# Building the slot table of a routed expert stage: 64 small indirect transfers, or one-hot rows summed by TensorE

## The chip, the cores and the metric

The kernel runs on one core of one Trainium2 chip. The metric is the device time of one execution in microseconds, median of several runs.

## The reference

The reference is a small language-model tower of two layers over 8 sequences of 512 tokens, with 256 features: an embedding, and in each layer an attention and a feed-forward block with experts. Only the second layer's feed-forward block matters here. Its arguments are 8 routed experts and one shared expert, all of the same form.

```
top-2 of the 8 router scores per token, with two gates (a softmax of the two scores)
y = x + shared(norm(x)) + sum over the token's two experts of gate * expert(norm(x))
expert(z) = (silu(z @ w1) * (z @ w3)) @ w2          z: 256, hidden: 512
```

The kernel does not compute every expert on every token. It sorts the 8192 (token, expert) pairs by expert into 72 tiles of 128 places, each expert beginning a new tile, and runs an expert on its tiles alone. The **slot table** says which token stands at place p of tile m, and a second table holds that pair's gate. A place without a pair holds a filler: a token number of 4096 or more, whose result is not added, and gate 0.

## The kernel before, in words

The five engines run programs of their own, written out by hand for each stage; semaphores order them, and between stages all engines meet. The stages of this block are three.

- **Routing** (`route`): normalizes all tokens, writes the normalized rows to device memory, computes the router's scores and the choice as one-hot rows `hot`, and the gates `first` and `second`. SP also writes a blank slot table to device memory here (`empty`, 72 fillers a partition).
- **Shared expert** (`shared_expert`): 16 steps of 256 tokens. On PE a step is `hidden(i)`, four blocks of 12 matmuls with 256 columns (reduced float32, in three passes of split operands) into the two halves of `psG`, and `down(i)`, 24 such matmuls into `psY`. ACT applies silu, DVE multiplies (line 2052) and splits, ACT rounds, and DVE adds `psY` to the residual in `add(i)` (line 2061). The order on PE is `hidden(i)`, `down(i-1)`, `hidden(i+1)`; on DVE `gated(i)`, `add(i-1)`, `gated(i+1)`. A block of `hidden` waits until DVE has multiplied the block two before it. Steps in the middle are loops of two steps on PE, ACT and DVE.
- Inside the shared expert, `Sort` computes on DVE, between steps, where each pair goes: `dve_scan` after `gated(0)`, `dve_slots` after `add(0)`, and `dve_plan` (which weights are due when) after `add(1)`. `dve_slots` ends in a cast of 64 slot numbers a partition to integers, `sloti`. POOL then sends 64 indirect transfers (`pool_scatter`, line 1824), each of which writes 128 entries (token, gate) of 8 bytes to their places of the table in device memory.
- **Routed experts** (`routed_experts`): SP first reads the table back (`listed`, line 2143) and then the first expert's weights (two transfers of 1.5 MB, line 2153). DVE copies `listed` as float32, PE transposes it, DVE writes `table` and `gate` (lines 2332 to 2336). Then 72 tiles: POOL gathers the tile's rows from device memory, PE turns them and multiplies by the expert's weights, and POOL adds the result into the output with an indirect transfer (line 2175), tile after tile.

At the start of the shared stage DVE waits for POOL's constants (`pool_constants`), and PE for DVE's `both`.

Of the kernel before, what the change touches and what calls it, by code (L numbers as in the profile page):

```python
# [17 lines left out]
P = 128  # L18
F32 = mybir.dt.float32
# [9 lines left out]
NT = B * S // P  # L29
# [1622 lines left out]
def ffn_swiglu(nc, a, res, ident, dram, s_soft):  # L1652
# [5 lines left out]
    with ExitStack() as ctx:  # L1658
# [3 lines left out]
        load_plan = k.sb("load_plan", [1, 2, E1N], I32)  # L1662
        with ExitStack() as ctx1:
# [5 lines left out]
            shared_expert(nc, a["out"], res, ident, xh, xl, hot, first, second, w_h, w_l, weights_due, weights_at, load_plan, dram, s_soft)  # L1669
        routed_experts(nc, a["out"], ident, weights_due, weights_at, load_plan, dram, s_soft)  # L1670


def route(nc, a, res, ident, xh, xl, hot, first, second, w_h, w_l, dram, s_soft):

    with ExitStack() as ctx:
# [4 lines left out]
        empty = k.sb("empty", [P, TILES, 2], I32)  # L1680
        s = {n: k.sem(n) for n in "raw hi wt bias share none filler empty blank".split()}
# [5 lines left out]
        def _(sp):  # L1687
# [6 lines left out]
            sp.wait_ge(s["empty"], 3)  # L1694
            sp.dma_start(dram["table"].rearrange("(p m) c -> p m c", p=P), empty[:]).then_inc(s["blank"], 16)
# [8 lines left out]
            sp.wait_ge(s["blank"], 17)  # L1704
            sp.wait_ge(turn.s["stored"], 16 * B + 1)

        @block.gpsimd
        def _(pool):
            split_weights(pool, [router.w], s["raw"], s["hi"], s["wt"])
            router.pool_names(pool)  # L1710
            pool.memset(none[:], 0.0).then_inc(s["none"], 1)

            pool.iota(empty[:, :, 0], [[0, TILES]], base=B * S, channel_multiplier=1).then_inc(s["empty"], 1)
            pool.memset(empty[:, :, 1], 0).then_inc(s["empty"], 1)
# [47 lines left out]
class Sort:  # L1762


    PAD = NT // 2

    def __init__(self, k, hot, gates, weights_due, weights_at, load_plan, dram, s_soft):
        self.hot, self.due, self.at, self.load_plan, self.dram, self.soft = hot, weights_due, weights_at, load_plan, dram, s_soft
# [13 lines left out]
        self.sloti = k.sb("sloti", [P, 2, NT], I32)  # L1782
# [9 lines left out]
        self.entry = k.sb("entry", [P, NT, 2, 2], I32)  # L1792
        self.gates = gates
        self.ps = k.ps("psS", [P, 2, NT * E])
        names = "fixed parts both ranked sorted ready slots".split()
        self.s = {n: k.sem("sort_" + n) for n in names}

    def pool_constants(self, pool):
# [38 lines left out]
    def dve_both(self, dve):  # L1837
        dve.wait_ge(self.s["parts"], 8)
        for n in range(2):
            dve.tensor_copy(self.entry[:, :, n, 1].bitcast(F32), self.gates[n][:]).then_inc(self.s["slots"], 1)  # L1840
# [29 lines left out]
    def dve_slots(self, dve, n):  # L1870
# [21 lines left out]
        dve.tensor_copy(self.sloti[:], self.slotf[:]).then_inc(s["slots"], 1)  # L1892
# [59 lines left out]
def shared_expert(nc, out, res, ident, xh, xl, hot, first, second, w_h, w_l, weights_due, weights_at, load_plan, dram, s_soft):  # L1952

    TT = 256
    NTT = B * S // TT
    with ExitStack() as ctx:
        k = Kit(nc, ctx, "ffn1b")
        sort = Sort(k, hot, (first, second), weights_due, weights_at, load_plan, dram, s_soft)
# [21 lines left out]
        def _(pool):  # L1980
            sort.pool_constants(pool)
            sort.pool_scatter(pool)

        @block.tensor
        def _(pe):
# [29 lines left out]
            with pe.Fori(0, NTT // 2 - 1) as i:  # L2015
                hidden(2 * i + 1, 1)
# [438 lines left out]
```

## Time and profile before

| what | value |
|---|---|
| median of 3 runs | 1915.01 us (1912.12 to 1915.68) |
| the profiled execution | 1910.06 us |
| its span, first to last instruction | 1908.2 us |
| mean granted TensorE clock | 0.863 of full speed |
| PE busy | 1335.6 us (70%) |
| DVE busy | 1011.3 us (53%) |
| POOL busy | 721.1 us (38%) |
| ACT busy | 635.0 us (33%) |

Times are microseconds from the start of the span. PE is TensorE's matmul, PEld its loading of weights, which overlaps PE; DVE is VectorE, ACT ScalarE, POOL GpSimd, SP the engine that issues most transfers. Busy time is the time in which an engine's instructions run; idle time in a row is what lay before the instruction, with the instruction that ended it. A busy share of the span says how much an engine does, and not whether anyone waits for it.

### The profile page before, as it was taken

The page shows a single profiled execution, that of the slowest core. Times are in us where ns is not written, and L with a number is a line of the kernel's source. Part 1 is how long each engine was busy: PE and PEld are TensorE (multiplying, and loading weights), DVE is VectorE, ACT ScalarE, POOL GpSimd, SP SyncE. Part 2 cuts the span into 40 slices and gives each one's busy share as a digit, 9 for nine tenths or more (in the row PEclk, how much of TensorE's full clock was granted, in tenths as well). Part 3 has the DMA queues.
Part 4 walks back from the last instruction along what each step waited for, and adds up shares of the span by engine and source line. Part 5 has one row for each costly group of instructions (what it writes and reads, how often), then busy time and mean ns, then how long its engine had stood idle before and what let it go on. Part 6 is the DMA issues. An engine that isn't in the chain of part 4 may idle for free. (4 is left out here: it accounts for less than half of the span.)

```text
span 1908.2 us, 32827 instructions
## 1 busy us (share of the span) xinstructions
PE 1335.6 (70%) x9797; PEld 1053.7 (55%) x9798; DVE 1011.3 (53%) x1870; ACT 635.0 (33%) x1271; POOL 721.1 (38%) x596
## 2 busy tenths in 40 slices
PE   0466646999999746534442399646699699999997
PEld 0255533555555544323331267534689578888886
DVE  0688854666767274557778255463544233333332
ACT  0032222565656412223221044212234234333342
POOL 6166662555554001113445500200174135444454
PEclk9788776999999878867766599867799899999999
DMA  1023337999998000023323254022001363444431
GB/s 28 18 77 111 112 114 154 246 252 256 244 255 227 7 6 0 0 61 110 110 78 100 64 113 92 10 83 76 10 25 33 120 216 55 115 113 115 112 55 26
DMA packets 161663, 190.87 MB, mean 100 GB/s; under 512 B 27028, under 2 KB 137052, under 8 KB 161604
## 3 DMA queue, kind: packets, MB, share of 16 engines
q1 hardware_dynamic: 133044, 129.24, 24.6%
q0 software_dynamic: 28560, 60.91, 12.7%
q8 instruction: 29, 0.48, 0.1%
q14 instruction: 30, 0.25, 0.0%
HBM read 112.89 MB, written 78.25 MB: 100 GB/s over the span
## 5 line engine op out<-in xcount | busy, mean ns | idle before, releaser
L1122 DVE TENSOR_REDUCE att_top<-att_psA 128x2 f32<-128x1024 f32 (+8 forms) x256 | 245.3, 986 | 186.4 <-PE att_psA L998 118.5
L1092 ACT ACTIVATE att_prob<-att_psB 128x512 f32<-128x512 f32 (+4 forms) x464 | 231.7, 536 | 137.4 <-PE att_psB L1017 71.3
L2175 POOL DMA_INDIRECT out<-ffn1c_y,ffn1c_table x72 | 114.2, 1585 | 179.8 <-ACT ffn1c_y L2288 106.0
L997 PE MATMUL att_psA<-att_ka,att_qa 96*128 96x384 bf16 (+3 forms) x512 | 126.3, 312 | 31.5 <-POOL att_mask_kNone L913 30.3
L1016 PE MATMUL att_psB<-att_qa,att_ka 98*128 98x256 bf16 (+3 forms) x512 | 128.0, 303 | 4.7 <-ACT att_prob L1092 2.2
L1050 PE MATMUL att_psO<-att_prob,att_vu 128*32 128x128 f32 (+7 forms) x1408 | 106.0, 405 | 35.1 <-ACT att_prob L1092 35.0
L2316 DVE TENSOR_TENSOR ffn1c_hid<-ffn1c_psG,ffn1c_sil 128x512 f32<-128x512 f32 x72 | 49.8, 691 | 144.4 <-PE ffn1c_psG L2216 144.4
L2216 PE MATMUL ffn1c_psG<-ffn1c_w_h,ffn1c_xh 128*128 x288 | 97.8, 421 | 10.8 <-DMA ffn1c_w_l<-experts_lo 3.8
L998 PE MATMUL att_psA<-att_mask_qNone,att_idb 128*128 128x128 bf16 x512 | 101.7, 226 | 0.0
L2164 POOL DMA_INDIRECT ffn1c_rows<-normed_rows,ffn1c_table x72 | 70.9, 984 | 78.0 <-DVE ffn1c_gate L2336 53.8
L1050 PEld LDWEIGHTS att_psO<-att_prob,att_vu 128*32 128x32 f32 x1408 | 51.1, 109 | 85.7 <-issue 64.1
L1017 PE MATMUL att_psB<-att_mask_kNone,att_idb 128*128 128x128 bf16 x512 | 98.2, 220 | 0.0
L532 PE MATMUL qkv_psQ<-qkv1p_w_qk_hi,qkv_xTh 128*128 128x512 f32 x64 | 28.9, 544 | 96.8 <-DVE qkv_xTl L703 96.8
L2216 PE MATMUL ffn1c_psG<-ffn1c_w_h,ffn1c_xl 128*128 x288 | 91.8, 401 | 0.0
L2216 PE MATMUL ffn1c_psG<-ffn1c_w_l,ffn1c_xh 128*128 x288 | 91.2, 398 | 0.0
L997 PEld LDWEIGHTS att_psA<-att_ka,att_qa 96*128 96x128 bf16 x512 | 50.9, 101 | 64.5 <-POOL att_mask_kNone L913 30.7
L1824 POOL DMA_INDIRECT slots<-ffn1b_entry,ffn1b_sloti x64 | 64.3, 1004 | 46.5 <-DVE ffn1b_sloti L1892 27.3
L1016 PEld LDWEIGHTS att_psB<-att_qa,att_ka 98*128 98x128 bf16 x512 | 49.8, 97 | 44.1 <-ACT att_prob L1092 25.1
L2307 DVE TENSOR_TENSOR ffn1c_xl<-ffn1c_psX,ffn1c_xh 128x256 fp32r<-128x256 f32 x72 | 30.5, 424 | 82.3 <-ACT ffn1c_xh L2266 82.3
L532 PEld LDWEIGHTS qkv_psQ<-qkv1p_w_qk_hi,qkv_xTh 128*128 128x128 f32 x64 | 16.7, 275 | 102.4 <-DVE qkv_xTl L703 98.9
L234 POOL CAST out_w_o_hi<-out_w_o_raw 128x512 fp32r<-128x512 f32 x2 | 1.2, 610 | 189.4 <-DMA out_w_o_raw<-in_w_o 189.4
L2280 ACT CAST ffn1c_hh<-ffn1c_psH 128x512 fp32r<-128x512 f32 x72 | 42.3, 587 | 88.4 <-PE ffn1c_psH L2227 88.4
(365 smaller groups left out, 3742.8 us busy)
## 6 DMA issues: line engine op xcount, KB each, us to landing
prep_raw<-in_w_all POOLq DMA_DIRECT2D x27, 512.0 KB, 6.9
experts_hi<-prep_hi POOLq DMA_DIRECT2D x27, 512.0 KB, 3.6
experts_lo<-prep_lo POOLq DMA_DIRECT2D x27, 512.0 KB, 4.3
ffn1c_w_h<-experts_hi SPq DMA_DIRECT2D x8, 1536.0 KB, 6.8
ffn1c_w_l<-experts_lo SPq DMA_DIRECT2D x8, 1536.0 KB, 11.0
qkv_near<-near_keys SPq DMA_DIRECT2D x32, 320.0 KB, 4.4
v_rows<-qkv_vaug SPq DMA_DIRECT2D x8, 1024.0 KB, 4.6
att_vu<-v_rows SPq DMA_DIRECT2D x32, 256.0 KB, 3.7
```

What stands on the lines that cost most here:

```text
L997: pe.matmul(out, q, ka[0:KROWS, u.buf, h, 0:cols], start=True, stop=True)
L998: return pe.matmul(out[:, cols - P:cols], idb[:], mask_q[w][:], start=False, stop=True, skip_group_check=True)
L1016: pe.matmul(out, keys, qs, start=True, stop=True)
L1017: return pe.matmul(out[:, 0:P], idb[:], mask_k[w][:], start=False, stop=True, skip_group_check=True)
L1050: mm = pe.matmul(psO[VW * h:VW * (h + 1), P * j:P * j + have], vu[:, v.buf, j, h, :], prob[:, v.par, h, j, 0:have], start=(j == 0), stop=( ...
L1092: act.activation(dst, src, ACT.Exp, scale=0.25).then_inc(s["exp"], 1)
L1122: dve.tensor_reduce(dst, src, AX.X, ALU.max).then_inc(s["max"], 1)
L1824: pool.indirect_dma_start(out=self.dram["table"], in_=self.entry[:, t, n, :], in_offset=None, out_offset=bass.IndirectOffsetOnAxis(ap=self ...
L2164: pool.indirect_dma_start(out=rows[:, t.buf, :], out_offset=None, in_=dram["rows"], in_offset=bass.IndirectOffsetOnAxis(ap=table[:, t.valu ...
L2175: pool.indirect_dma_start(out=rows_out, in_=y[:, t.buf, :], in_offset=None, out_offset=bass.IndirectOffsetOnAxis(ap=table[:, t.value:t.val ...
L2216: mm = pe.matmul(psG[:, t.par, g, :], x[:, t.par, P * c:P * (c + 1)], w[:, bass.ds(at, 1), col:col + F1], start=(q == 0), stop=(q == 5))
L2316: dve.tensor_tensor(hid[:, t.par, :], psG[:, t.par, 1, :], sil[:, t.par, :], ALU.mult).then_inc(s["act"], 1)
```

## The change

The slot table no longer passes through device memory. Every pair's slot is split into a tile number `high` and a lane `low` (slot = 128 x tile + lane; rounding is done by adding and taking off a large constant). For each of the 64 columns of pairs DVE makes a one-hot row of 128 lanes and a one-hot row of 72 tiles, and multiplies the tile row by the token number (less 4096) and by the gate. PE multiplies the two and sums over all columns into one tile of PSUM, `psE`, 128 lanes by 2 x 72; DVE then adds 4096 and writes `table` and `gate`. This is done in 8 parts of 8 columns: DVE makes part 0 after `add(1)` and parts 1 to 7 after `add(3)` to `add(9)`, PE sums part c between `hidden(c+5)` and `down(c+4)`, and DVE reads the sum after `add(12)`. The plan moves from behind `add(1)` to behind `add(2)`.

Taken out are the blank table and its transfer in the routing stage, POOL's 64 transfers, the reading back, and the two transposes with their copies. POOL makes two more constants. The loops of the shared stage on PE and DVE are written out; ACT's stays.

The diff, cut to its core:

```diff
 class Sort:
     PAD = NT // 2
+    PART = 8
+    PARTS = 2 * NT // PART
+    WHOLE = 12582912.0
...
-        pool.iota(self.entry[:, :, :, 0], [[P, NT], [0, 2]], base=0, channel_multiplier=1).then_inc(s["parts"], 1)
-        pool.wait_ge(s["parts"], 8)
-
-    def pool_scatter(self, pool):
-        pool.wait_ge(self.s["slots"], 4)
-        for t in range(NT):
-            for n in range(2):
-                pool.indirect_dma_start(out=self.dram["table"], in_=self.entry[:, t, n, :], in_offset=None,
-                                        out_offset=bass.IndirectOffsetOnAxis(ap=self.sloti[:, n, t:t + 1], axis=0)
-                                        ).then_inc(self.soft["entries"], 16)
-        pool.wait_ge(self.soft["entries"], 16 * 2 * NT)
+        pool.iota(self.entry[:, :, 0], [[0, 2], [P, NT]], base=-B * S, channel_multiplier=1,
+                  allow_small_or_imprecise_dtypes=True).then_inc(s["parts"], 1)
+        pool.iota(self.lanes[:], [[1, P]], base=0, channel_multiplier=0,
+                  allow_small_or_imprecise_dtypes=True).then_inc(s["parts"], 1)
+        pool.iota(self.tiles[:], [[1, TILES]], base=0, channel_multiplier=0,
+                  allow_small_or_imprecise_dtypes=True).then_inc(s["parts"], 1)
+        pool.wait_ge(s["parts"], 10)
+
+    def dve_held(self, dve, c):
+        at = slice(self.PART * c, self.PART * (c + 1))
+        shape = [P, self.PART, TILES]
+        if c >= 1:
+            dve.wait_ge(self.s["held"], c + 1)
+        dve.tensor_tensor(self.tile_hot[:], self.tiles[:].unsqueeze(1).to_broadcast(shape),
+                          self.high[:, 2, at].unsqueeze(2).to_broadcast(shape), ALU.is_equal).then_inc(self.s["tile"], 1)
+        if c >= 2:
+            dve.wait_ge(self.s["placed"], c)
+        shape = [P, self.PART, P]
+        dve.tensor_tensor(self.lane_hot[:, c % 2], self.lanes[:].unsqueeze(1).to_broadcast(shape),
+                          self.low[:, at].unsqueeze(2).to_broadcast(shape), ALU.is_equal).then_inc(self.s["lane"], 1)
+        dve.wait_ge(self.s["tile"], c + 2)
+        shape = [P, self.PART, 2, TILES]
+        dve.tensor_tensor(self.held[:, c % 2], self.tile_hot[:].unsqueeze(2).to_broadcast(shape),
+                          self.entry[:, at, :].unsqueeze(3).to_broadcast(shape), ALU.mult).then_inc(self.s["held"], 1)
+
+    def pe_place(self, pe, c):
+        pe.wait_ge(self.s["lane"], c + 2)
+        pe.wait_ge(self.s["held"], c + 2)
+        for n in range(self.PART):
+            mm = pe.matmul(self.psE[:].rearrange("p v m -> p (v m)"), self.lane_hot[:, c % 2, n, :],
+                           self.held[:, c % 2, n].rearrange("p v m -> p (v m)"), start=(c == 0 and n == 0),
+                           stop=(c == self.PARTS - 1 and n == self.PART - 1), skip_group_check=True)
+        mm.then_inc(self.s["placed"], 1)
+
+    def dve_table(self, dve):
+        dve.wait_ge(self.s["placed"], self.PARTS + 1)
+        dve.tensor_scalar(self.table[:], self.psE[:, 0, :], float(B * S), None, ALU.add).then_inc(self.s["ready"], 1)
+        dve.tensor_copy(self.gate[:], self.psE[:, 1, :]).then_inc(self.s["ready"], 1)
+        dve.wait_ge(self.s["ready"], 6)
...
-        dve.tensor_copy(self.sloti[:], self.slotf[:]).then_inc(s["slots"], 1)
+        slot = self.slotf[:].rearrange("p c t -> p (c t)")
+        dve.tensor_scalar(self.high[:, 0], slot, 1.0 / P, 0.5 / P - 0.5, ALU.mult, ALU.add).then_inc(s["slots"], 1)
+        dve.wait_ge(s["slots"], 4)
+        dve.tensor_scalar(self.high[:, 1], self.high[:, 0], self.WHOLE, None, ALU.add).then_inc(s["slots"], 1)
+        dve.wait_ge(s["slots"], 5)
+        dve.tensor_scalar(self.high[:, 2], self.high[:, 1], -self.WHOLE, None, ALU.add).then_inc(s["slots"], 1)
+        dve.wait_ge(s["slots"], 6)
+        dve.scalar_tensor_tensor(self.low[:], self.high[:, 2], -float(P), slot, ALU.mult, ALU.add).then_inc(s["slots"], 1)
+        dve.wait_ge(s["slots"], 7)
...
 def shared_expert
...
+    LATE = 5
...
             hidden(0, 0)
-            with pe.Fori(0, NTT // 2 - 1) as i:
-                hidden(2 * i + 1, 1)
-                down(2 * i, 0)
-                hidden(2 * i + 2, 0)
-                down(2 * i + 1, 1)
-            hidden(NTT - 1, 1)
-            down(NTT - 2, 0)
+            for i in range(1, NTT):
+                hidden(i, i % 2)
+                if 0 <= i - LATE < sort.PARTS:
+                    sort.pe_place(pe, i - LATE)
+                down(i - 1, 1 - i % 2)
             down(NTT - 1, 1)
...
             gated(2, 0)
             add(1, 1)
-            sort.dve_plan(dve, n)
-            with dve.Fori(1, NTT // 2 - 1) as i:
-                gated(2 * i + 1, 1)
-                add(2 * i, 0)
-                gated(2 * i + 2, 0)
-                add(2 * i + 1, 1)
-            gated(NTT - 1, 1)
-            add(NTT - 2, 0)
+            sort.dve_held(dve, 0)
+            for i in range(3, NTT):
+                gated(i, i % 2)
+                add(i - 1, 1 - i % 2)
+                if i == 3:
+                    sort.dve_plan(dve, n)
+                if 1 <= i - LATE + 2 < sort.PARTS:
+                    sort.dve_held(dve, i - LATE + 2)
+                if i == LATE + sort.PARTS:
+                    sort.dve_table(dve)
             add(NTT - 1, 1)
...
 def routed_experts
...
-            sp.dma_start(listed[:], dram["table"].rearrange("(m p) c -> m p c", p=P)).then_inc(s["listed"], 16)
...
-            pe.wait_ge(s["slots"], 3)
-            for c in range(2):
-                mm = pe.transpose(psX[:, P * c:P * c + TILES], slots[:, c, :], ident[0:TILES, 0:TILES])
-            mm.then_inc(s["slotsT"], 1)
-            pe.wait_ge(s["table"], 3)
...
-            dve.wait_ge(s["listed"], 17)
-            dve.tensor_copy(slots[:, 0, :], listed[:, :, 0]).then_inc(s["slots"], 1)
-            dve.tensor_copy(slots[:, 1, :], listed[:, :, 1].bitcast(F32)).then_inc(s["slots"], 1)
-            dve.wait_ge(s["slotsT"], 2)
-            dve.tensor_copy(table[:], psX[:, 0:TILES]).then_inc(s["table"], 1)
-            dve.tensor_copy(gate[:], psX[:, P:P + TILES]).then_inc(s["table"], 1)
-            dve.wait_ge(s["table"], 3)
```

## Rows read from the trace of the kernel before

**Rows 1.** Windows: PE, PEld, DVE, ACT, POOL busy us, granted clock, DMA share, GB/s.
```profile
1349.00:1504.50 155.50, 145.43 (x1154) 143.44 (x1154) 71.74 (x187) 56.14 (x136) 64.27 (x64) 0.96 0.09 26
1504.50:1523.20 18.70, 1.84 (x7) 0.90 (x7) 2.27 (x7) 0.74 (x2) 5.77 (x6) 0.60 0.62 222
...
1375.30:1377.00 1.70, 1.67 (x14) 1.67 (x15) 0.76 (x2) 1.07 (x4) 1.09 (x1) 1.00 0.00 0
...
1390.00:1392.00 2.00, 2.00 (x12) 2.00 (x11) 0.76 (x2) 0.61 (x2) 1.39 (x3) 0.50 0.01 1
```

**Rows 2.** View of line 1824, POOL: instructions, duration, first and last start.
```profile
L1824 POOL DMA_INDIRECT slots<-ffn1b_entry,ffn1b_sloti x64: 963/967/1379, 1375.8 to 1458.3; - x64
```

**Rows 3.** Chain that ended last, in order of time: start, length, what.
```profile
1511.50 11.44 DMA ffn1c_w_l<-experts_lo
...
1557.84 6.90 DMA ffn1c_w_h<-experts_hi
...
1649.56 10.93 DMA ffn1c_w_l<-experts_lo
```

**Rows 4.** Timeline of DVE, shared stage: start, length, instruction, idle before and releaser.
```profile
1371.33 0.69 DVE L2061 TENSOR_TENSOR m_res<-m_res,ffn1b_psY 128x512 f32<-128x512 f32 x1 [1.58 <-PE ffn1b_psY L2007]
...
1374.85 0.42 DVE L2052 TENSOR_TENSOR ffn1b_act_f<-ffn1b_psG,ffn1b_sil 128x256 f32<-128x256 f32 x1
...
1381.41 0.69 DVE L2061 TENSOR_TENSOR m_res<-m_res,ffn1b_psY 128x512 f32<-128x512 f32 x1 [1.45 <-PE ffn1b_psY L2007]
...
1382.16 0.74 DVE L1912 TENSOR_TENSOR ffn1b_past<-ffn1b_ends,ffn1b_number 1x576 f32<-1x576 f32 x1
1382.83 0.20 DVE L1913 TENSOR_TENSOR ffn1b_pick<-ffn1b_ends,ffn1b_number 1x64 f32<-1x64 f32 x1
...
1386.72 0.22 DVE L1944 TENSOR_TENSOR ffn1b_which<-ffn1b_which,ffn1b_rounds 1x72 f32<-1x72 f32 x1
...
1387.80 0.42 DVE L2052 TENSOR_TENSOR ffn1b_act_f<-ffn1b_psG,ffn1b_sil 128x256 f32<-128x256 f32 x1 [0.45 <-DVE ffn_load_plan L1948]
...
1466.48 0.69 DVE L2061 TENSOR_TENSOR m_res<-m_res,ffn1b_psY 128x512 f32 x1 [1.48 <-PE ffn1b_psY L2007]
1468.92 0.42 DVE L2052 TENSOR_TENSOR ffn1b_act_f<-ffn1b_psG,ffn1b_sil 128x256 f32<-128x256 f32 x1 [1.76 <-ACT ffn1b_sil L2033]
...
1475.54 0.69 DVE L2061 TENSOR_TENSOR m_res<-m_res,ffn1b_psY 128x512 f32 x1 [1.48 <-PE ffn1b_psY L2007]
...
1484.12 0.69 DVE L2061 TENSOR_TENSOR m_res<-m_res,ffn1b_psY 128x512 f32 x1 [1.48 <-PE ffn1b_psY L2007]
```

**Rows 5.** Timeline of PE, shared stage.
```profile
1375.33 0.51 PE L1995 MATMUL ffn1b_psG<-ffn1s_xh,ffn1s_w_h 128*128 x2 [1.24 <-DVE ffn1b_act_f L2052]
...
1388.28 0.51 PE L1995 MATMUL ffn1b_psG<-ffn1s_xh,ffn1s_w_h 128*128 x2 [4.12 <-DVE ffn1b_act_f L2052]
...
1392.76 0.63 PE L2007 MATMUL ffn1b_psY<-ffn1s_w_h,ffn1b_act_h 128*128 128x256 f32 x4
...
1466.15 0.40 PE L1995 MATMUL ffn1b_psG<-ffn1s_xh,ffn1s_w_h 128*128 x2
```

**Rows 6.** Timeline of SP's queue at the start of the expert stage.
```profile
1509.59 0.34 SPq L2143 DMA_DIRECT2D ffn1c_listed<-slots  x1
1511.01 0.40 SPq L2153 DMA_DIRECT2D ffn1c_w_h<-experts_hi  x1
```

**Rows 7.** Timeline of POOL, then DVE, at the start of the shared stage.
```profile
1347.95 0.16 POOL L1812 IOTA ffn1b_thresholds<- 128x32 f32 x1
...
1348.20 0.28 POOL L1817 IOTA ffn1b_entry<- 128x64 int32 x1
...
1348.51 0.20 DVE L1840 COPY ffn1b_entry<-ffn_first 128x32 f32<-128x32 f32 x1 [4.41 <-POOL ffn1b_entry L1817]
```

**Rows 8.** Timeline of PE's weight loads in the embedding stage.
```profile
54.27 0.19 PEld L164 LDWEIGHTS emb_psO<-emb_w_blk,emb_rowsT 128*128 128x128 f32 x1 [0.24 <-issue]
54.70 0.19 PEld L164 LDWEIGHTS emb_psO<-emb_w_blk,emb_rowsT 128*128 128x128 f32 x1 [0.24 <-issue]
```

More of the change, by code:

```diff
@@ L1662, in ffn_swiglu @@
         load_plan = k.sb("load_plan", [1, 2, E1N], I32)
+        table, gate = k.sb("table", [P, TILES], I32), k.sb("gate", [P, TILES])
         with ExitStack() as ctx1:
@@ L1668, in ffn_swiglu @@
             route(nc, a, res, ident, xh, xl, hot, first, second, w_h, w_l, dram, s_soft)
-            shared_expert(nc, a["out"], res, ident, xh, xl, hot, first, second, w_h, w_l, weights_due, weights_at, load_plan, dram, s_soft)
-        routed_experts(nc, a["out"], ident, weights_due, weights_at, load_plan, dram, s_soft)
+            shared_expert(nc, a["out"], res, ident, xh, xl, hot, first, second, w_h, w_l, table, gate, weights_due, weights_at, load_plan, s_soft)
+        routed_experts(nc, a["out"], ident, table, gate, weights_due, weights_at, load_plan, dram, s_soft)
 def route(nc, a, res, ident, xh, xl, hot, first, second, w_h, w_l, dram, s_soft):
@@ L1679, in route @@
         none = k.sb("none", [P, D])
-        empty = k.sb("empty", [P, TILES, 2], I32)
-        s = {n: k.sem(n) for n in "raw hi wt bias share none filler empty blank".split()}
+        s = {n: k.sem(n) for n in "raw hi wt bias share none filler".split()}
         router.weights_there = s["wt"], 2
@@ L1791, in __init__ @@
         self.plan = k.sb("plan", [1, 2, E])
-        self.entry = k.sb("entry", [P, NT, 2, 2], I32)
+        self.entry = k.sb("entry", [P, 2 * NT, 2])
         self.gates = gates
         self.ps = k.ps("psS", [P, 2, NT * E])
-        names = "fixed parts both ranked sorted ready slots".split()
+        self.psE = k.ps("psE", [P, 2, TILES])
+        names = "fixed parts both ranked sorted ready slots lane tile held placed".split()
         self.s = {n: k.sem("sort_" + n) for n in names}
@@ L1837, in dve_both @@
     def dve_both(self, dve):
-        dve.wait_ge(self.s["parts"], 8)
+        dve.wait_ge(self.s["parts"], 10)
         for n in range(2):
-            dve.tensor_copy(self.entry[:, :, n, 1].bitcast(F32), self.gates[n][:]).then_inc(self.s["slots"], 1)
+            dve.tensor_copy(self.entry[:, NT * n:NT * (n + 1), 1], self.gates[n][:]).then_inc(self.s["slots"], 1)
         dve.tensor_tensor(self.both[:], self.hot[:, 0], self.hot[:, 1], ALU.add).then_inc(self.s["both"], 1)
@@ L2115, in step_walk, with routed_experts @@
         stage(Step(0, n))
-def routed_experts(nc, out, ident, weights_due, weights_at, load_plan, dram, s_soft):
+def routed_experts(nc, out, ident, table, gate, weights_due, weights_at, load_plan, dram, s_soft):
     assert TILES % 4 == 0
@@ L2123, in routed_experts @@
         k = Kit(nc, ctx, "ffn1c")
-        listed, slots = k.sb("listed", [TILES, P, 2], I32), k.sb("slots", [TILES, 2, P])
-        table, gate = k.sb("table", [P, TILES], I32), k.sb("gate", [P, TILES])
         rows = k.sb("rows", [P, 4, D])
@@ L2133, in routed_experts @@
         psX, psH, psY = (k.ps(n, [P, 512]) for n in ("psX", "psH", "psY"))
-        s = {n: k.sem(n) for n in "listed slots slotsT table w xT xTh xTl gate sil act hT hTh hTl y ys".split()}
+        s = {n: k.sem(n) for n in "w xT xTh xTl gate sil act hT hTh hTl y ys".split()}
         k.open([(s["act"], 1), (s["gate"], 2), (s["y"], 1), (s["hT"], 1)])
@@ L2182, in stage @@
                 scatter(t - 2)
-            pool.wait_ge(s["table"], 2)
             for n in range(3):
@@ L2295, in stage @@
                 output(t - 2)
-            act.wait_ge(s["table"], 3)
             high_rows(Step(0, 0))
@@ L2348, in second_ffn_space @@
         w_lo=nc.dram_tensor("experts_lo", (pieces, P, CUT), F32).ap(),
-        rows=nc.dram_tensor("normed_rows", (B * S + P, D), F32).ap(),
-        table=nc.dram_tensor("slots", (TILES * P, 2), I32).ap())
+        rows=nc.dram_tensor("normed_rows", (B * S + P, D), F32).ap())
     sem = lambda name: ctx.enter_context(nc.semaphore(name))
     soft = dict(raw=[sem(f"piece_loaded{n}") for n in range(2)], stored=[sem(f"piece_stored{n}") for n in range(2)],
-                entries=sem("entries"), shared=sem("shared_weights"), got=[sem(f"rows_got{n}") for n in range(4)],
+                shared=sem("shared_weights"), got=[sem(f"rows_got{n}") for n in range(4)],
                 placed=[sem(f"rows_placed{n}") for n in range(4)])
```

22 lines of the change are left out of this document (11 added, 11 removed).

## The prediction

> **What bounds the kernel now.** I read four views, from coarse to fine. The page's first part gives shares of the whole span, PE's 70% the largest, and an average of that kind says nothing about an edit to one stage; the stretches around the change have to be cut out. The windows cut at the stage edges show two of them [rows 1]. In the shared stage (155.5 us) PE is busy 145.4 us, DVE 71.7 and POOL 64.3: this stage ends when PE ends. Between it and the first expert matmul lie 18.7 us in which PE does 1.8 us of work. The expert stage follows. The view of POOL's line names its part: 64 transfers into the slot table, 1.0 us each, the last of them begun at 1458.3 us [rows 2]. The stage's PE work ends at about 1504.5 us, so POOL is through some 45 us before anyone could miss it. The chain of waits, read from its start, is the fourth view: after the shared stage it runs over the first load of expert weights, 11.44 us from its issue at 1511.50, and not over the table, although the table is read back in the same gap [rows 3]. The reader should see two things here: the 64 transfers that the change removes are covered by PE's work, and the reading back is covered by a weight load.
>
> **What bounds a step of the shared stage.** A step is a hidden (48 matmuls in four blocks) and a down (24). DVE's adds, one per step, come 8.58 us apart in short steps (1475.54 to 1484.12) and 9.06 in long ones (1466.48 to 1475.54) [rows 4]; 8.58 over 72 matmuls is 0.12 us each. PE may run two blocks of a hidden ahead of DVE (the two halves of psG); the third waits for DVE's first product of that step. From the rows: hidden starts 0.33 us before DVE's add (1466.15, 1466.48), its third block is due 24 matmuls or 2.88 us later, that is 2.55 after the add's start, and it starts 0.48 us after DVE's product (1374.85, 1375.33). With D the time from DVE's add to its next product, PE therefore loses D - 2.07 us. The two long cases fit: D is 3.52 behind the slots work (1371.33 to 1374.85), which gives a loss of 1.45, and PE shows 1.24 idle, the rest being the drain of its last matmul; D is 6.39 behind the plan (1381.41 to 1387.80), a loss of 4.32, and PE shows 4.12 [rows 4, 5]. In long steps D is 2.44 (1466.48 to 1468.92), and the row names ACT's silu as what DVE waits for: it comes late at the head of ACT's own loop, which is not edited.
>
> **The change part by part.**
> Removed: POOL's 64 transfers. Value 0, since PE's work hides them by 45 us; were that cover gone they would be worth at most the 82.5 us from first to last [rows 2].
> Removed: the reading back. DVE's two copies, PE's two transposes and two more copies follow the read's issue at 1509.59, and all of them fall in the time of the weight load, which is under way until 1522.9 [rows 3, 6]. What is on the path is one issue on SP's queue ahead of the weights: 0.34 us. The bound on the other side is all the time from that issue to the weights' issue, 1509.59 to 1511.01, 1.42 us, but SP reads the load plan in it and still must. The gathers start earlier, which the weight load hides as well, since the chain runs over the weights: 0 too. I take -0.35, bounds 0 and -1.4. The blank table's write and its wait in the routing stage leave a queue (SP's) that the stage's DVE does not wait for: 0.
> Added on POOL: two iotas of 128 and 72 columns before the constants are ready, and DVE then PE wait for exactly these (DVE idle 4.41 us up to 1348.51 [rows 7]). An iota of 64 columns took 0.28 us and one of 32 took 0.16, so 3.75 ns a column and 0.04: 0.52 and 0.31, less some 0.05 each that neighbours overlap: +0.7, bounds 0.3 (two of 0.16) and 1.0.
> Added on DVE in the slots work: four small operations, each waiting for the one before, in place of one cast. One of 72 columns in such a chain takes 0.22 [rows 4]; three more are +0.65, bounds 0.4 and 1.0. PE already waits there (1.24 idle), so all of it is on the path.
> Added on DVE, eight times: three operations of 576, 1024 and 1152 elements a partition between an add and the next product. 576 elements with spread operands take 0.74 and start their successor after 0.67 (1382.16, 1382.83 [rows 4]), so I take 0.07 off each length; 256 take 0.42 and 512 take 0.69, so 1.05 ns an element, which makes the add 0.62 and the operations of 1024 and 1152 elements 1.16 and 1.29. D becomes 0.62 + 0.67 + 1.16 + 1.29 = 3.74. That is 1.67 us lost in a step that lost nothing, and 3.74 - 2.44 = 1.30 more in a long one. The parts follow the adds 1 and 3 to 9, so they hit hiddens 3, 5, 7, 9, 11 and the long 6, 8, 10; the plan moves from hidden 3 to hidden 4 and costs its 4.32 there, where 0.37 was lost before. Together 5 x 1.67 + 3 x 1.30 - 0.37 = 11.9. DVE is idle for most of a step, but this work stands in the one place of its order that PE waits behind, so the idle time does not hide it. Bounds: 10 if each operation is 5% cheaper, 13 if a wait adds 0.15 to each part.
> Queued behind the waits that the parts add: DVE's for `held` and `placed` are met a step earlier, and so is PE's for `lane` and `held`: part c is made after add c+2 and used after hidden c+5.
> Added on PE, 64 matmuls in plain float32 with 144 columns, 8 in each of eight steps, between hidden and down, where PE is the bound. The trace has no such shape. Its plain float32 matmuls with 512 columns are two instructions each (32 for 16 calls), one every 0.43 us at full pace [rows 8], which is 0.84 ns a column. At 144 columns that is 0.121; beside it stands 0.012, by which this stage's matmul of 256 columns (0.119) exceeds its columns at half of 0.84 ns (0.107). 128 x 0.133 = 17.0 us. Lower bound 128 x 0.121 = 15.5. Upper: each instruction waits for its own weights, 0.19 each [rows 8], 24.3. I take 17.0, the nearest row in kind; there the load of 0.19 lies under the matmul.
> Added after the last part: two operations on the result at hidden 14, D about 1.3, under 2.07: 0. More semaphores to open in one stage, fewer in two: 0.
> Written-out loops: in the rows the only gap in the steady steps is the one at ACT's late silu, which lies in the middle of the PE and DVE loop bodies (an even hidden) and not at their edge. So 0. The Trainium skill, Runtime: NRT & Kernel Launch, section on instruction fetch mechanics, says that a taken branch out of the fetched pages stalls its engine and that kernels therefore gain by unrolling. By that rule the seven edges would have stalls to give back; the trace does not agree, for its long steps are the even ones. Taken at the whole difference of 0.48 us, the rule would make the sum 3.4 us smaller.
>
> **Sum.** 0.7 + 0.65 + 11.9 + 17.0 - 0.35 = 29.9 us. The profiled execution took 1910.06 us (1908.2 of span), which gives 1940.0. The median shown is 1915.01, 4.95 higher; against it the same sum gives 1944.9 us, 1.5% slower.
>
> **Rivals.**
> The DVE parts are hidden: something lets PE run on (the first product needs less time behind the parts than I think). For it: DVE is idle more than half the stage. Against: both measured cases follow D - 2.07. Then 1944.9 - 11.9 = 1933.0.
> The clock falls at each stall. After the wait of 4.12 us PE went from 2.4 to 1.2 GHz (the window from 1390 to 1392 shows 0.50 [rows 1]), and the two blocks due in 2.88 us took from 1388.28 to 1392.76, 4.48 [rows 5]: a cost of 1.6. Eight would add 12.8: 1957.7. Against it: after 1.24 us idle the clock stayed at 2.4 GHz (the window from 1375.3 to 1377 shows 1.00 [rows 1]), and 1.4 is what the parts leave. The slots stall grows to 1.9 us idle, so one such fall is possible.
> The experts' weights come sooner, which is the way to no loss. The chain has three waits on weights in the expert stage, 11.44, 6.90 and 10.93 us, 29.3 together [rows 3]. If earlier gathers emptied the queues so that all three vanished, the result would be 1944.9 - 29.3 = 1915.6, no change. It decides only if it gives back nearly all (26 or more): the first load moves 3 MB that nothing but its issue can hasten, and the plan of the other two is the same.
> PE pays for every weight load: 24.3 in place of 17.0, 1952.2. It is inside my range.
>
> **Chances.** My sum 0.66, with the dearer matmuls 0.08 more; parts hidden 0.10; clock falls 0.12; the weights come sooner 0.02; something else that leaves it within or below 0.2% 0.02. A measurement of this kernel tells about 0.2% (3.8 us) from no change. The range goes from below the hidden case to above the clock case, 1930 to 1961. Faster 0.02, same 0.02, slower 0.96.
>
> **What would show it.** In the profile after: 128 matmul instructions of 144 columns, about 17 us busy, one every 0.13 us; PE idle 1.4 us in the third block of eight hiddens, released by DVE's product; the plan's 4 us idle one hidden later; steps with both parts about 12.4 us apart against 8.6 to 9.06; the first weight load issued about 0.3 us sooner after the stage before; the expert stage as long as it was. It would be wrong if DVE's parts overlapped with nothing waiting, if the float32 matmuls had a price beyond 0.12 to 0.19 us, or if the clock fell at the stalls.

## The result, and the profile after

The changed kernel takes 1937.56 us (median of 4 runs, 1936.06 to 1940.40); the kernel before took 1915.35 in the same comparison (4 runs, 1912.12 to 1919.12). The ratio is 1.0119 with a 95% interval of 1.0101 to 1.0137: 22.2 us slower, where the prediction said 29.9. Run again on one chip beside the first experiments, it was 1939.2 against 1913.48, ratio 1.0127 (1.0107 to 1.0147). The profiled execution took 1936.06 us with a span of 1934.2, that is 26.0 above that of before.

First the windows of the changed kernel, cut at the first matmul of the shared stage, its last add, the first expert matmul and the end. The columns are those of [rows 1].

```profile
1350.81:1532.87 182.06, 161.88 (x1282) 159.04 (x1282) 96.22 (x215) 56.19 (x136) 0.00 (x0) 0.97 0.07 23
1532.87:1550.95 18.08, 1.35 (x5) 0.58 (x5) 1.54 (x3) 0.75 (x2) 5.83 (x6) 0.60 0.61 232
1550.95:1934.20 383.25, 359.95 (x2156) 313.40 (x2156) 129.21 (x214) 140.13 (x286) 180.23 (x138) 0.98 0.43 102
```

Cut at the same four events, the kernel before gives 155.29, 18.64 and 385.02 us. The shared stage grew by 26.8, PE's busy time in it by 16.5 and DVE's by 24.6; the gap shrank by 0.56. The first window is the firm number: the second profile of the changed kernel has 182.15 there. The expert stage is not: in the fourteen profiles of this document, whose kernels do not differ in it, it takes 382.4 to 387.8 us. What comes before the shared stage scatters more, since that stage begins between 1348.4 and 1356.5 us. This is why the medians (22 and 26 us) and the stretches (26.2) agree only that far.

DVE's timeline in the changed kernel answers to [rows 4], in the columns of that group:

```profile
1372.61 0.69 DVE L2100 TENSOR_TENSOR m_res<-m_res,ffn1b_psY 128x512 f32<-128x512 f32 x1 [1.49 <-PE ffn1b_psY L2048]
...
1376.70 0.23 DVE L1931 SCALAR_TENSOR_TENSOR ffn1b_low<-ffn1b_high,ffn1b_slotf 128x64 f32<-128x64 f32 x1
1376.96 0.42 DVE L2091 TENSOR_TENSOR ffn1b_act_f<-ffn1b_psG,ffn1b_sil 128x256 f32<-128x256 f32 x1
...
1383.52 0.69 DVE L2100 TENSOR_TENSOR m_res<-m_res,ffn1b_psY 128x512 f32<-128x512 f32 x1 [1.44 <-PE ffn1b_psY L2048]
...
1387.20 0.42 DVE L2091 TENSOR_TENSOR ffn1b_act_f<-ffn1b_psG,ffn1b_sil 128x256 f32<-128x256 f32 x1
...
1393.73 0.69 DVE L2100 TENSOR_TENSOR m_res<-m_res,ffn1b_psY 128x512 f32<-128x512 f32 x1 [1.44 <-PE ffn1b_psY L2048]
...
1398.35 0.15 DVE L1980 TENSOR_SCALAR ffn1b_plan<-ffn1b_plan 1x8 f32<-1x8 f32 x1
...
1399.45 0.42 DVE L2091 TENSOR_TENSOR ffn1b_act_f<-ffn1b_psG,ffn1b_sil 128x256 f32<-128x256 f32 x1
...
1419.68 0.69 DVE L2100 TENSOR_TENSOR m_res<-m_res,ffn1b_psY 128x512 f32<-128x512 f32 x1 [3.41 <-PE ffn1b_psY L2048]
1420.28 0.75 DVE L1834 TENSOR_TENSOR ffn1b_tile_hot<-ffn1b_tiles,ffn1b_high 128x576 f32<-128x576 f32 x1
1420.95 1.22 DVE L1839 TENSOR_TENSOR ffn1b_lane_hot<-ffn1b_lanes,ffn1b_low 128x1024 f32<-128x1024 f32 x1
1422.09 1.35 DVE L1843 TENSOR_TENSOR ffn1b_held<-ffn1b_tile_hot,ffn1b_entry 128x1152 f32<-128x1152 f32 x1
1423.36 0.41 DVE L2091 TENSOR_TENSOR ffn1b_act_f<-ffn1b_psG,ffn1b_sil 128x256 f32<-128x256 f32 x1
```

D, the time from the start of an add to the start of the next product, is 4.35 us behind the slots work, 3.68 behind a part, and 5.72 behind the plan. The three operations of a part follow one another without idle time, and the next product follows them.

PE's timeline answers to [rows 5]:

```profile
1377.44 0.50 PE L2036 MATMUL ffn1b_psG<-ffn1s_xh,ffn1s_w_h 128*128 128x256 f32 x2 [2.07 <-DVE ffn1b_act_f L2091]
...
1411.65 0.51 PE L2036 MATMUL ffn1b_psG<-ffn1s_xh,ffn1s_w_h 128*128 128x256 f32 x2 [1.38 <-DVE ffn1b_act_f L2091]
...
1414.62 2.12 PE L1850 MATMUL ffn1b_psE<-ffn1b_held,ffn1b_lane_hot 128*128 128x144 f32 x16
...
1423.83 0.39 PE L2036 MATMUL ffn1b_psG<-ffn1s_xh,ffn1s_w_h 128*128 128x256 f32 x1 [1.38 <-DVE ffn1b_act_f L2091]
```

PE sits idle 2.07 us behind the slots work and 1.38 in every step with a part; 16 instructions of 144 columns stand ahead of eight of the downs. Behind the wait of 2.07 us the granted clock stayed at 1.00. The chain at the stage's end, SP's queue, and POOL's two new iotas with the DVE copy that waits for them answer to [rows 3], [rows 6] and [rows 7]:

```profile
1539.36 11.35 DMA ffn1c_w_l<-experts_lo
...
1538.85 0.40 SPq L2191 DMA_DIRECT2D ffn1c_w_h<-experts_hi  x1
...
1349.65 0.23 POOL L1823 IOTA ffn1b_lanes<- 128x128 f32 x1
1349.85 0.18 POOL L1825 IOTA ffn1b_tiles<- 128x72 f32 x1
...
1350.06 0.18 DVE L1872 COPY ffn1b_entry<-ffn_first 128x32 f32<-128x32 f32 x1 [4.95 <-POOL ffn1b_tiles L1825]
```

The chain still runs over the first load of weights, 11.35 us.

### The profile page after: what moved, and what is told of

It is laid out like the page before. It is cut to its first block and busy times, and to the rows that moved or that the text cites. A ratio compares the mean times of both kernels' runs of the same rounds, so it can differ in the third digit from the quotient of the medians.

```text
span 1934.2 us, 32783 instructions
## 1 busy us (share of the span) xinstructions
PE 1348.6 (70%) x9923; PEld 1066.2 (55%) x9924; DVE 1035.4 (54%) x1895; ACT 635.4 (33%) x1271; POOL 659.4 (34%) x532
## 5 line engine op out<-in xcount | busy, mean ns | idle before, releaser
L2213 POOL DMA_INDIRECT out<-ffn1c_y,ffn_table x72 | 114.3, 1588 | 178.8 <-ACT ffn1c_y L2320 89.3
L2202 POOL DMA_INDIRECT ffn1c_rows<-normed_rows,ffn_table x72 | 71.7, 996 | 213.1 <-POOLq L79 188.6
L384 POOL TENSOR_TENSOR qkv_rot<-qkv_qk,qkv_sin 128x256 f32<-128x256 f32 x64 | 63.0, 1012 | 23.2 <-ACT qkv_qk L351 19.0
L2036 PE MATMUL ffn1b_psG<-ffn1s_xh,ffn1s_w_h 128*128 128x256 f32 x256 | 55.1, 298 | 20.1 <-DVE ffn1b_act_f L2091 20.1
```

Source lines behind the costliest of these rows:

```text
L384: ins = pool.tensor_tensor(dst[:, :, u, :], src[:, :, 1 - u, :], sn, ALU.mult)
L2202: pool.indirect_dma_start(out=rows[:, t.buf, :], out_offset=None, in_=dram["rows"], in_offset=bass.IndirectOffsetOnAxis(ap=table[:, t.valu ...
L2213: pool.indirect_dma_start(out=rows_out, in_=y[:, t.buf, :], in_offset=None, out_offset=bass.IndirectOffsetOnAxis(ap=table[:, t.value:t.val ...
```

## The experiments

All of them were timed beside the kernel before. The first eight ran on one chip, where it took 1913.5 and 1914.3 us; the last four on another, where it took 1986.2, of which more below. The changed kernel itself did not run on the second chip: what is said to lie above or below it there compares across the chips. "Shared stage" is always the stretch from the first matmul of that stage to its last add: 155.3 us before, 182.1 changed.

**The changed kernel again.** No edit.

> The changed kernel unedited, as a yardstick beside the next three. Theory A (the loss is a sum on PE's path: eight waits behind DVE's parts, about 10 us, and 128 matmul instructions, about 16 us, with small terms around them): 26 us above the kernel before when traced stretch by stretch, so a median 22 to 27 us above it, and in the trace steps of 12.18 us. Theory B (the removed transfers and the reading back had a value of some 4 us that the stretches do not show): the median stays near 22 while the stretches again add up to 26.

1939.2 us, 25.7 above the kernel before; shared stage 182.15, steps of 12.18 us, the gap 18.07, the expert stage 386.21. Theory A's numbers hold; theory B is not needed for the difference of the medians, since the stages that were not edited differ by more than 4 us between profiles.

**The parts ahead of the add.** Part 0 is moved ahead of `add(1)` in the same way.

```diff
-                add(i - 1, 1 - i % 2)
                 if 1 <= i - LATE + 2 < sort.PARTS:
                     sort.dve_held(dve, i - LATE + 2)
+                add(i - 1, 1 - i % 2)
```

> The changed kernel with each DVE part made ahead of the add instead of behind it, in the time in which DVE waits for PE's down. Theory A: the waits of 1.38 us idle on PE, eight of them, vanish, and D from add to the next product falls back to 1.48 or 2.44 us; the time falls by about 10 us (4 x 1.61 + 3 x 1.2 + part of the eighth), to about 12 to 16 us above the kernel before. Rival 1 (the parts merely hold DVE, and PE's waits come from elsewhere in the chain of ACT and DVE): no change against the changed kernel. Rival 2: the add itself comes late by the 3 us of the part and PE waits for psY or for the products instead; gain under 4 us.

1928.44 us, 10.8 below the changed kernel, ratio to before 1.0085 (1.0066 to 1.0104); shared stage 170.07, so 12.0 shorter. One step of DVE's timeline of this kernel:

```profile
1425.31 0.75 DVE L1834 TENSOR_TENSOR ffn1b_tile_hot<-ffn1b_tiles,ffn1b_high 128x576 f32<-128x576 f32 x1
1425.97 1.22 DVE L1839 TENSOR_TENSOR ffn1b_lane_hot<-ffn1b_lanes,ffn1b_low 128x1024 f32<-128x1024 f32 x1
1427.11 1.35 DVE L1843 TENSOR_TENSOR ffn1b_held<-ffn1b_tile_hot,ffn1b_entry 128x1152 f32<-128x1152 f32 x1
1428.79 0.69 DVE L2100 TENSOR_TENSOR m_res<-m_res,ffn1b_psY 128x512 f32<-128x512 f32 x1 [0.33 <-PE ffn1b_psY L2048]
1430.16 0.42 DVE L2091 TENSOR_TENSOR ffn1b_act_f<-ffn1b_psG,ffn1b_sil 128x256 f32<-128x256 f32 x1 [0.68 <-PE ffn1b_psG L2036]
```

The same three operations now lie where DVE would wait for PE's down, the add is 0.33 us after their end, and D is 1.37. PE has no idle time over 0.5 us in these steps. Nothing was taken away but a place in the order, and 12 us went: this term is a wait and not DVE's throughput, and both rivals of this run fall.

**Every one-hot matmul twice.**

```diff
+            for copy in (1, 0):
-            mm = pe.matmul(self.psE[:]..., self.lane_hot[...], self.held[...], ...)
+                mm = pe.matmul(self.psE[:, copy]..., self.lane_hot[...], self.held[...], ...)
```

> The changed kernel with each of the 64 one-hot matmuls issued a second time, into a second half of psE that nobody reads. Theory A: PE is the bound there, so 128 more instructions add what the first 128 cost: 15.9 us (16 in 1.99 us, eight times), and steps of 12.18 become 14.2. Rival (the matmuls lie partly under waits that PE has anyway, or cost their weight load when alone): an addition under 8 us, or over 20.

1957.37 us, 18.2 above the changed kernel; shared stage 197.14, 15.1 longer; steps of 14.13 to 14.15 in place of 12.18. The view of the line shows twice the instructions at the same length:

```profile
L1851 PE MATMUL ffn1b_psE<-ffn1b_held,ffn1b_lane_hot x256: 283/286/287, 1418.9 to 1520.4; 128*128 128x144 f32 x128
```

1.97 us for 16 instructions is 0.123 each, and 128 of them are 15.8 us. The eight steps that hold them grew by 15.7 together; the start of the stage ran 0.6 shorter. They hide under nothing, and their weight loads of 0.19 us lie under the matmuls. The other 3 of the 18.2 us are not theirs: they stand in the stages that were not edited.

**The removed work put back beside the new.** The copy of the table is not used.

```diff
+        for q in range(2 * NT):
+            pool.indirect_dma_start(out=old, in_=self.entry[:, q, :], ...)
...
+            sp.dma_start(listed[:], dram["old"].rearrange("(m p) c -> m p c", p=P)).then_inc(s["listed"], 16)
```

> The changed kernel with the removed work put back beside the new: the blank table, POOL's 64 indirect transfers (which write a copy of the table that nobody uses), and SP's read of 72 KB ahead of the experts' weights, plus the cast of 64 slot numbers. Theory A: covered work, worth 0.1 us for the cast and 0.3 to 0.6 for SP's issue; the time is within 0.1% of the changed kernel. Theory B: it is slower than the changed kernel by some 4 us, which was the value of the removal.

1943.11 us, ratio to before 1.0154 (1.0134 to 1.0174), and for the changed kernel beside it 1.0127 (1.0107 to 1.0147): the intervals overlap, 3.9 us between the medians. The trace finds 1.8 of it: the shared stage 182.93 and the gap 18.97. Of the 0.9 in the shared stage 0.1 is the cast (D behind the slots work 4.46 in place of 4.35). Some 0.7 is the clock: it fell behind the wait after the slots work, which cost 1.5, and it reached full speed earlier at the start of the stage, which gave back 0.8. That is not the transfers' work, for the kernel with the reading back alone shows the same fall without them (below). The third is one row in DVE's plan, which carries a quarter of a microsecond; it is the operation of line 1980 above (0.15 us), and in this kernel, while POOL sends, it is

```profile
1400.34 0.37 DVE L1994 TENSOR_SCALAR ffn1b_plan<-ffn1b_plan 1x8 f32<-1x8 f32 x1
```

The kernel before has it at 0.38. It is not POOL's sending alone, though: in the kernel before with the sorting work ahead of the adds, the same operation takes 0.15 us while POOL sends (line 1940, at 1385.00). D behind the plan is 5.96 here and 5.72 without the transfers.

**The loops written out, in the kernel before.**

DVE's loop; PE's is written out in the same way.

```diff
-            with dve.Fori(1, NTT // 2 - 1) as i:
+            for i in range(3, NTT):
+                gated(i, i % 2)
+                add(i - 1, 1 - i % 2)
```

> The kernel before with the loops of the shared stage written out on PE and DVE and nothing else changed. Theory A: DVE's entry into its loop goes (0.45 us of DVE idle ahead of hidden 3's first product, then 6.39 becomes 5.7), worth 0.7 us; the steps stay at 8.58 and 9.06: within 0.1% of the kernel before. Rival (a taken branch stalls the engine at each edge): 3 us or more faster, and steps of 8.58 all through.

1912.41 us against 1914.32, ratio 0.9990 (0.9981 to 0.9998); shared stage 154.56, so 0.7 shorter. The steps stay at 8.58 and 9.02 (9.06 before), D behind the plan goes from 6.39 to 5.98: DVE's entry into its loop cost 0.4. The prediction weighed a rule of the Trainium skill here (Runtime: NRT & Kernel Launch, section on instruction fetch mechanics), by which an edge whose branch leaves the fetched pages would have a stall to give back. The trace shows none on PE: its steps are the same with and without the edges. Whether any of these branches leaves the fetched pages, no run here shows.

**The sorting work ahead of the adds, in the kernel before.** With the loops written out as in the last one.

```diff
-            add(0, 0)
             n = sort.dve_slots(dve, n)
+            add(0, 0)
             gated(2, 0)
-            add(1, 1)
             sort.dve_plan(dve, n)
+            add(1, 1)
```

> The kernel before with written-out loops, and with the slots work and the plan each moved from behind DVE's add to ahead of it. Theory A (what stands between an add and the next product is PE's loss beyond 2.07 us, and what stands ahead of the add is free up to the 1.5 us that DVE waits there): the slots stall of 1.24 us goes, the plan's 4.12 shrinks to about 2.7, so 3 us faster than the kernel before, perhaps 1.6 more if a fall of PE's clock goes with it. Rival: the add now comes late and down waits for psY, nothing gained.

1909.51 us, ratio 0.9978 (0.9965 to 0.9991): 4.8 below the kernel before, so 0.2% faster, and faster than the changed kernel too. The shared stage is 150.03. PE's idle times of 1.24 and 4.12 us in [rows 5] have become, in PE's timeline,

```profile
1376.39 0.50 PE L1995 MATMUL ffn1b_psG<-ffn1s_xh,ffn1s_w_h 128*128 128x256 f32 x2 [0.19 <-DVE ffn1b_act_f L2048]
...
1387.24 0.51 PE L1995 MATMUL ffn1b_psG<-ffn1s_xh,ffn1s_w_h 128*128 128x256 f32 x2 [2.02 <-DVE ffn1b_act_f L2048]
```

Against the kernel with the loops written out the two waits are 2.7 us shorter, and the fall of the clock behind the plan (1.5 us) is gone: behind the wait of 2.02 us the granted clock is 1.00. The stage is 4.5 us shorter.

**Reduced-float32 one-hot matmuls.** Gates in two summands, 216 columns, one instruction a matmul.

```diff
+        self.lane_hot = k.sb("lane_hot", [P, 2, self.PART, P], F32R)
+        self.held = k.sb("held", [P, 2, self.PART, 3, TILES], F32R)
```

> The changed kernel with the 64 one-hot matmuls in reduced float32: gates in two summands, so 216 columns in place of 144, one instruction each in place of two; the third operation of a DVE part grows from 1152 to 1728 elements. Theory A: PE's term falls from 15.9 us to 64 x 0.10 to 0.12, about 7, and DVE's part grows by 0.6 us, which eight waits pay in full: +4.8; net 4 us faster than the changed kernel. Rival (the price goes by instruction or weight load and not by passes of columns): 64 x 0.19 = 12, net 1 us slower.

1944.49 us, 5 above the changed kernel, where 4 below was expected; shared stage 185.68. The matmuls did what they should: a step with full clock is 11.62 us, 0.56 less than 12.18, although D is 4.28 (0.6 more), so eight matmuls take about 0.8 and one about 0.10. But five of the seven steps take 13.1 to 13.2. Two windows of this kernel, one in a step of 11.62 and one in a step of 13.11:

```profile
1430.00:1433.00 3.00, 3.00 (x28) 3.00 (x27) 1.56 (x5) 1.77 (x6) 0.00 (x0) 1.00 0.01 3
1455.00:1458.00 3.00, 3.00 (x18) 3.00 (x17) 1.51 (x4) 1.30 (x5) 0.00 (x0) 0.55 0.00 0
```

In the second PE's granted clock is 0.55, so it spends most of it at 1.2 GHz. The longer part leaves PE idle for 1.98 us in place of 1.38, and after that wait the clock falls in five of eight cases: it stays at 2.4 GHz in the two steps of 11.6 and at hidden 3, whose step is 10.82.

**Both: reduced matmuls, and parts ahead of the adds.**

> Reduced-float32 matmuls, and the parts ahead of the adds. Theory A: both gains, and the growth of DVE's part now lies in its idle time: about 10 us for the waits and 8 to 9 for the matmuls below the changed kernel, so some 5 to 8 us above the kernel before. Rival: DVE's part of 3.6 us no longer fits ahead of the add and gives part of it back, 10 us above the kernel before.

1922.06 us, ratio to before 1.0047 (1.0031 to 1.0063); shared stage 161.99, steps of 9.29 and 9.8 to 9.9. With no wait behind the parts there is no fall of the clock there, and the cheap matmuls show their worth.

**A part made longer, the matmuls as they were.**

```diff
+        shape = [P, self.PART, 64]
+        dve.tensor_tensor(self.spare[:], self.tiles[:, 0:64]..., self.low[:, at]..., ALU.is_equal)
```

> The changed kernel with a fourth DVE operation of 512 elements in each of the eight parts, whose result nobody reads; the one-hot matmuls stay in plain float32. It makes the part as long as that of the reduced-float32 kernel (D 4.28 us, PE idle 1.98), in which PE's clock fell in most steps. Theory A (the clock falls because the idle time is longer, 1.98 against 1.38 us): 8 x 0.6 = 4.8 us from D alone and about 1.6 for each fall, five of seven: some 12 us above the changed kernel, with steps of 12.8 and of 14.4. Rival (it fell because of the other kind of matmul, or of its shorter time): the clock stays, all steps 12.8, and 4.8 us above the changed kernel.

1954.46 us; shared stage 194.2, 12.1 above the changed kernel. The steps are 12.78 or 14.2 to 14.3. PE's timeline at one long step and one short step, and windows inside both:

```profile
1432.82 0.55 PE L2041 MATMUL ffn1b_psG<-ffn1s_xh,ffn1s_w_h 128*128 128x256 f32 x2 [1.99 <-DVE ffn1b_act_f L2096]
...
1447.10 0.50 PE L2041 MATMUL ffn1b_psG<-ffn1s_xh,ffn1s_w_h 128*128 128x256 f32 x2 [1.98 <-DVE ffn1b_act_f L2096]
...
1433.00:1436.00 3.00, 3.00 (x16) 3.00 (x17) 1.22 (x4) 1.25 (x5) 0.00 (x0) 0.52 0.00 0
...
1449.00:1451.00 2.00, 2.00 (x19) 2.00 (x18) 1.35 (x4) 0.91 (x4) 0.00 (x0) 1.00 0.03 8
```

The idle time is the same in both, 1.98 us; after the one the clock is 0.52, after the other 1.00. It fell after five of the eight waits (hidden 3 among them: 12.26 for a step that would be 10.8). So the longer idle time is enough, and the kind of matmul is not needed. Over all profiles: after 1.38 us idle the clock fell in none of 47 waits (six profiles), after 1.95 to 2.18 us in 14 of 28 (twelve profiles, the waits of the slots work and of the plan included). The rival "the clock falls at each stall" begins to hold between the two. The idle time alone does not decide it, since the same 1.98 us was followed by a fall in ten cases and by none in six; what does is open.

**All sorting work ahead of the adds.** The kernel with both, and the slots work and the plan moved as well.

> The kernel with reduced-float32 matmuls and the parts ahead of the adds, and the slots work and the plan ahead of their adds as well. Theory A: it gains what the same move gained in the kernel before, 4 to 5 us of the shared stage, from 162.0 to about 157.5 us against 155.3 before, so 1916 to 1918 us, 0.1 to 0.2% above the kernel before. Rival: the parts already use the idle time ahead of the adds, the move gains under 2 us.

1918.50 us; shared stage 159.27, 2.7 below the kernel with both and 4 above the kernel before. That lies between the two theories, and not for the rival's reason: no part stands in the plan's step. PE's waits, in its timeline,

```profile
1373.75 0.51 PE L2043 MATMUL ffn1b_psG<-ffn1s_xh,ffn1s_w_h 128*128 128x256 f32 x2 [0.27 <-DVE ffn1b_act_f L2098]
...
1393.84 0.50 PE L2043 MATMUL ffn1b_psG<-ffn1s_xh,ffn1s_w_h 128*128 128x256 f32 x2 [1.95 <-DVE ffn1b_act_f L2098]
```

went from 2.07 to 0.27 us behind the slots work and from 3.43 to 1.95 behind the plan. With a fall of the clock that cost 0.3 less (it fell behind the plan in both), the move gave 3.6 us. Of these 0.9 were lost again up to the end of the first down, where PE waits as long as in the kernel with both (3.07 and 3.06 us) but has a granted clock of 0.79 in place of 0.82. Its ratio to the kernel before on that chip says nothing on this, for the reason that comes next.

**The reading back alone, and the transfers alone.** The last two kernels are the changed one with one half each of the removed work put back beside the new.

> The changed kernel with only the blank table and SP's read of 72 KB ahead of the experts' weights put back (not POOL's transfers). Theory A: the gap from the last add to the first expert matmul grows by 0.5 to 0.9 us, and nothing else: the same time as the changed kernel within 0.1%. Theory B: it carries the 2 to 4 us that the kernel with everything put back lay above the changed one.

> The changed kernel with only the blank table, the cast and POOL's 64 transfers put back (not the read). Theory A: D behind the slots work 0.11 longer, D behind the plan 0.25 longer (one small DVE operation takes 0.37 in place of 0.15 us while POOL sends), perhaps one fall of the clock more, 1.6: 0.4 to 2 us in the shared stage. Theory B: 4 us, in stretches outside the shared stage.

The reading back alone: 1941.02 us, shared stage 182.64, gap 19.64 (18.08 without; 18.97 with everything put back), so it costs 0.9 to 1.6 us of gap and not 0.35. The shared stage has no transfers in it, and PE's wait behind the slots work is that of the changed kernel, but here the clock fell behind it:

```profile
1377.27 0.50 PE L2049 MATMUL ffn1b_psG<-ffn1s_xh,ffn1s_w_h 128*128 128x256 f32 x2 [2.07 <-DVE ffn1b_act_f L2104]
...
1378.00:1381.00 3.00, 3.00 (x18) 3.00 (x17) 1.52 (x4) 1.41 (x5) 0.00 (x0) 0.55 0.00 0
```

The transfers alone: 2012.2 us, with the kernel before at 1986.2 on the same chip. Neither theory had that. Windows of the transfers' own 78 us, of the kernel with the transfers alone on this chip and, second, of the kernel with everything put back on the first chip:

```profile
1383.00:1461.00 78.00, 22.28 (x109) 19.59 (x108) 8.13 (x15) 3.71 (x10) 59.40 (x62) 0.59 0.03 5
```

```profile
1383.00:1461.00 78.00, 67.42 (x541) 66.12 (x540) 46.26 (x99) 21.90 (x53) 60.62 (x58) 0.98 0.10 25
```

POOL does the same 59 to 61 us of work in both; PE does 22.3 us in the one and 67.4 in the other. PE's timeline on the second chip:

```profile
1411.57 0.27 PE L2063 MATMUL ffn1b_psY<-ffn1s_w_h,ffn1b_act_h 128*128 128x256 f32 x1 [1.13 <-issue]
1413.67 0.37 PE L2063 MATMUL ffn1b_psY<-ffn1s_w_h,ffn1b_act_h 128*128 128x256 f32 x1 [1.82 <-issue]
1415.80 0.37 PE L2063 MATMUL ffn1b_psY<-ffn1s_w_h,ffn1b_act_h 128*128 128x256 f32 x1 [1.75 <-issue]
...
1419.30 0.37 PE L2063 MATMUL ffn1b_psY<-ffn1s_w_l,ffn1b_act_h 128*128 128x256 f32 x1 [2.22 <-issue]
1420.70 0.37 PE L2063 MATMUL ffn1b_psY<-ffn1s_w_l,ffn1b_act_h 128*128 128x256 f32 x1 [1.03 <-issue]
1423.50 0.37 PE L2063 MATMUL ffn1b_psY<-ffn1s_w_l,ffn1b_act_h 128*128 128x256 f32 x1 [2.43 <-issue]
1426.30 0.37 PE L2063 MATMUL ffn1b_psY<-ffn1s_w_l,ffn1b_act_h 128*128 128x256 f32 x1 [2.43 <-issue]
```

PE waits up to 3.8 us between two matmuls of one group, for "issue", that is for nothing that the profile shows; before and after the transfers it runs as ever, and the shared stage is 256.3 us, 73 longer than with everything put back on the first chip. On this chip the nine runs of the kernel before took 1982.6 to 1987.3 us, 72 above the first chip in the median, and the three kernels run beside it that lack the 64 transfers were at 1918, 1941 and 1954, near what their stages say. So here the design without the 64 transfers was the faster one. The expert stage's 144 indirect transfers (72 gathers, 72 adds) do no such thing on the second chip: the stage takes 382.7 us there. Why POOL's 64 transfers stop PE on one chip and not on the other is open: the traces show no releaser, and the kernel before was not profiled there. The two chips were also used at different times, so that it is the chip, and not something else that differed, is not shown.

## Why the prediction was right, and where its numbers were off

It said slower, from a sum on PE's path, and the sum's two large terms were what the runs found.

- **The 64 transfers covered by PE's work: 0.** In the first comparison the traces give up to 0.3 us (the plan's operation that takes 0.38 while POOL sends). The first chip bears the 0 out; on the second the cover did not exist. The prediction had priced that loss of cover at up to 82.5 us without a mechanism; 73 were measured there.
- **The reading back: -0.35.** The gap fell by 0.56, and grew by 0.9 to 1.6 when the read was put back. Right that the weight load covers it, mis-sized by some tenths to one microsecond.
- **POOL's iotas: +0.7.** DVE's copy starts 2.41 us after POOL's first operation (1347.65) against 2.18 before: +0.23. An iota of 128 columns takes 0.23 us and one of 72 takes 0.18; the slope came from an integer iota of 64 columns, which in float32 takes 0.18.
- **The slots work: +0.65.** +0.83, D 4.35 against 3.52: the four operations take 0.94 from the first's start to the next product (1376.02 to 1376.96), and the cast that they replace held its successor for only 0.11 (1374.74 to 1374.85), where the prediction took 0.22 for each.
- **The parts: +11.9.** D was forecast at 3.74 and is 3.68, PE idle 1.4 and is 1.38. With the slack of 2.07 as before, and 2.48 for a long step without a part, 5 x 1.61 + 3 x 1.20 - 0.37 is 11.3, and moving the parts gave back 12.0.
- **The matmuls: +17.0.** 15.8: 0.123 us an instruction and not 0.133. The lower bound, columns alone, was nearly it.
- **Left out: -0.7.** D behind the plan fell from 6.39 to 5.72, 0.4 of it for DVE's loop entry, which the prediction put at 0 with the loops. The rest is the plan's one operation, 0.15 us in place of 0.38, which the runs tie to POOL's sending only in part.

0.23 + 0.83 + 11.3 + 15.8 - 0.56 - 0.7 = 26.9; the trace has 26.8 - 0.56 + 0.23 = 26.4. So of the 7.7 us by which 29.9 exceeded the first comparison's 22.2, 3 to 3.5 are terms mis-sized, the largest the matmuls' 1.2. The rest fits the scatter of the stages that were not edited: the second comparison gave 25.7.

Of the rivals, "the parts are hidden" was wrong for this order and right for the order that held it ahead of the add. "The clock falls at each stall" was wrong at 1.38 us idle and right in ten of 16 steps at 1.98, so the forecast stood 0.6 us from it. The one fall that the prediction held possible, behind the slots work, did not come in the changed kernel's two profiles at 2.07 us; it came in three of the ten profiles that have this wait, so leaving it out of the sum was in part luck. "The weights come sooner" did not happen: 11.35 us in place of 11.44.

The forecast also owes something to where it was measured. It named what the transfers would be worth without their cover, but gave that no chance of its own. Had the two kernels met on the second chip, "slower" would, by all that the last four runs show, have been wrong.

## What to carry to other kernels

Busy shares did not price this change; the place in the order did. Work put between a buffer's release and the next product cost PE each microsecond beyond its slack of 2.07, and the same work put where the engine waits anyway cost nothing: measure D against the slack before asking how busy the engine is. A wait that leaves TensorE idle for 2 us in place of 1.4 can cost 1.5 more through its clock, so a cheaper matmul bought with a longer stall may lose.

## What was not expected of the hardware

- After 1.98 us of idle time PE went to 1.2 GHz in 10 of 16 cases, after 1.95 to 2.18 us in 14 of 28 with these among them, after 1.38 us in none of 47. In steps that are otherwise alike a fall cost 1.4 to 1.6 us.
- A matmul in plain float32 with 144 columns is two instructions of 0.123 us; in reduced float32 with 216 columns it is one of about 0.10.
- A DVE operation of 8 elements on one partition takes 0.15 us, and 0.37 to 0.38 at one place while POOL issues indirect transfers, in three profiles; in a fourth it takes 0.15 while POOL issues them, and with the plan behind the transfers' end it takes 0.15 as well.
- On one of two chips, POOL's 64 indirect transfers of 128 entries of 8 bytes held PE to 22 us of work in 78; on the other PE did 67 us of work in the same stretch.
